# Two state-space scans: rows of B for all sixteen states through TensorE and VectorE, none through the DMA and GpSimd

## The chip, the cores and the metric

The program runs on one core of a Trainium2 chip. The metric is the device time of one execution in microseconds, and the median of three runs is given. The core's engines are TensorE (PE), VectorE (DVE), ScalarE (ACT) and GpSimd (POOL); SyncE (SP) issues DMAs. Each engine works through its own queue in order, and the queues meet at semaphores only.

## What is computed

A decoder of twelve blocks over 16 sequences of 128 rows by 256 columns. Two of the blocks hold a selective scan, and the change touches those two only. Their core, from the reference of the second (`L3_attn`), for every feature f, state n of 16 and row l:

```
A_bar = jnp.exp(-Delta[..., None] * A)
BX = (Delta * h)[..., None] * Bm[:, :, None, :]
_, states = jax.lax.associative_scan(comb, (A_bar, BX), axis=1)    # s[l] = A_bar[l] * s[l-1] + BX[l]
y = jnp.einsum('blfn,bln->blf', states, Cm) + D * h
```

The first (`L1_attn`, a Mamba block with 512 inner features) computes the same kind of scan. B and C are, for every row, 16 numbers each that all features share.

## The kernel before

All twelve blocks are stages of one program. Stage `mamba` (the first scan) works on 4 groups of 4 sequences; a group has 4 blocks of 128 features, taken two at a time as a unit, and each unit goes through the 16 states, so that there are 4 x 2 x 16 = 128 steps. Stage `sequence_ssm` (the second scan) has 256 features, one unit for each of 4 groups, so 64 steps. A step N is, for 128 partitions and two feature blocks of 512 columns:

- `decay` (ACT, L1225): two exponentials; three buffers.
- the drive, dt*x times the row of B. In three steps out of four: `brow` (PE, L1205) spreads the row of B over all partitions into a PSUM bank, with a bf16 matmul against `select`, and `drive` (DVE, L1237) multiplies into another pair of PSUM banks, `c.twins[1]`. In every fourth step (`SHARE = 4`, `shared`): `bload` (SP, L1174) fetches the row by a DMA that repeats it on 128 partitions into `bcol`, and `offer` (POOL, L1261) multiplies into the SBUF tile `offer`.
- `scan` (DVE, L1250): the recurrence over 1024 columns, from decay and drive into one of four `state` buffers. It waits for `summed(N-4)`.
- `crow` (SP, L1169): the row of C by DMA into `ccol`, four buffers; `weigh` (POOL, L1265): state times the row of C, in place.
- `sum` (PE, L1214): adds the weighted state into y, through the identity; four matmul records for a step. The unit's first `sum` also adds the skip term (L1211) and waits for the `finish` of the unit before (`gated`). `finish` (DVE, L1477 and L1780) multiplies y by the gate.

Beside the steps each group needs side work: norm, transposes, projections, the convolution, softplus, and for the group before it the output projection. Its matmuls go through the `side` banks (`Planned`), filled in order; PE waits before it fills a bank again until ACT or DVE has emptied it. The eight PSUM banks are: 0 and 1 for y, 2 and 3 for the drive, 4 for rows of B (one bank), 5 to 7 for side products.

What sets the order: each kind of step has a due number (`MAMBA_BY_STEP` and so on), in units of a step, and `as_due` sorts all of them. Every engine then runs its own share of that list in that order. So a number compares two pieces of work on one engine, not across engines. A bank for rows of B is refilled after the `drive` that reads it (`Fills.before`).

## Time and profile before

| | us |
|---|---|
| median of 3 runs | 3886.33 |
| lowest, highest | 3883.37, 3897.04 |
| the profiled execution | 3884.58 |
| its span in the trace | 3883.2 |
| first scan, first to last scan instruction | 1258.95 to 1808.03 |
| second scan, first to last scan instruction | 3156.74 to 3457.31 |

The profile is of one execution. It has the busy time of each engine, tables of instructions by line with the idle time before them, waits by releaser, and instructions in order of time. A row of a table by line gives the count, total busy time and mean duration in ns, and after the second bar the engine's idle time just before these instructions with what ended it. A row in order of time gives start, duration, engine, line, the operation, how many instructions it merges, and in brackets the idle time before the first. Matmul ends are modelled, and POOL spans are rough.

### The profile page before, as it was taken

The page shows a single profiled execution, that of the slowest core. Times are in us where ns is not written, and L with a number is a line of the kernel's source. Part 1 is how long each engine was busy: PE and PEld are TensorE (multiplying, and loading weights), DVE is VectorE, ACT ScalarE, POOL GpSimd, SP SyncE. Part 2 cuts the span into 40 slices and gives each one's busy share as a digit, 9 for nine tenths or more (in the row PEclk, how much of TensorE's full clock was granted, in tenths as well). Part 3 has the DMA queues.
Part 4 walks back from the last instruction along what each step waited for, and adds up shares of the span by engine and source line. Part 5 has one row for each costly group of instructions (what it writes and reads, how often), then busy time and mean ns, then how long its engine had stood idle before and what let it go on. Part 6 is the DMA issues. An engine that isn't in the chain of part 4 may idle for free. (4 is left out here: it accounts for less than half of the span.)

```text
span 3883.2 us, 52620 instructions
## 1 busy us (share of the span) xinstructions
PE 3058.4 (79%) x17435; PEld 1956.1 (50%) x17435; DVE 2296.3 (59%) x6354; ACT 1543.6 (40%) x3513; POOL 1642.5 (42%) x1169
## 2 busy tenths in 40 slices
PE   6989996878942877865899999478879667768798
PEld 4666665656621332322666666245656423235665
DVE  6998984374333898886244343544542259975553
ACT  4776763211212444431344444315612134426521
POOL 4777774103443888786122222300020157870020
PEclk8999998888976998988999999688969879889999
DMA  3000000202442222222000000111031222220000
GB/s 101 6 10 7 10 10 26 124 22 86 123 119 101 74 68 79 77 74 64 1 8 1 1 1 1 19 71 42 9 120 31 58 75 64 60 79 1 2 1 22
DMA packets 105943, 179.54 MB, mean 46 GB/s; under 512 B 32656, under 2 KB 62376, under 8 KB 102928
## 3 DMA queue, kind: packets, MB, share of 16 engines
q1 hardware_dynamic: 96128, 150.08, 11.9%
q0 software_dynamic: 9552, 26.10, 2.7%
q8 instruction: 148, 2.42, 0.3%
q14 instruction: 115, 0.94, 0.1%
HBM read 151.62 MB, written 24.51 MB: 45 GB/s over the span
## 5 line engine op out<-in xcount | busy, mean ns | idle before, releaser
L1265 POOL TENSOR_TENSOR L_attn_state<-L_attn_state,L_attn_ccol 128x1024 f32<-128x1024 f32 x192 | 533.2, 2791 | 114.5 <-DVE L_attn_state L1250 114.3
L1214 PE MATMUL bank<-L_attn_state,ident 128*128 128x512 f32 x768 | 430.0, 690 | 141.2 <-POOL L_attn_state L1265 140.3
L1225 ACT ACTIVATE L_attn_decay<-L_attn_dt,L_attn_A 128x512 f32<-128x512 f32 x384 | 253.4, 713 | 320.8 <-DVE L_attn_state L1250 291.1
L1214 PEld LDWEIGHTS bank<-L_attn_state,ident 128*128 128x128 f32 x768 | 155.1, 215 | 367.3 <-POOL L_attn_state L1265 224.8
L1250 DVE TENSOR_TENSOR_SCAN L_attn_state<-L_attn_decay,bank 128x1024 f32<-128x1024 f32 x144 | 328.7, 2283 | 14.4 <-ACT L_attn_decay L1225 1.0
L1107 POOL TENSOR_TENSOR L_xattn_prob<-L_xattn_prob,L_xattn_inv 128x1024 f32<-128x1024 f32 x64 | 121.2, 1893 | 408.5 <-DVE L_xattn_inv L1090 408.5
L1237 DVE TENSOR_TENSOR bank<-L_attn_dtx,bank 128x1024 f32<-128x1024 f32 x144 | 175.8, 1221 | 75.2 <-PE bank L1205 55.8
L2831 POOL TENSOR_TENSOR L_attn_t<-L_attn_t,L_attn_base 128x1024 f32<-128x1024 f32 x96 | 182.6, 1902 | 37.7 <-DVE L_attn_base L2780 36.9
L758 ACT ACTIVATE L_xattn_prob<-bank,L_xattn_top 128x128 f32<-128x128 f32 x512 | 142.3, 377 | 56.3 <-DVE L_xattn_top L807 56.0
L2835 POOL TENSOR_TENSOR L_attn_t<-L_attn_t 128x512 f32<-128x512 f32 x96 | 122.1, 1272 | 96.3 <-ACT L_attn_t L2639 96.3
L1032 ACT ACTIVATE L_xattn_prob<-L_xattn_masked,L_xattn_low 128x256 f32<-128x256 f32 x256 | 128.1, 506 | 83.5 <-DVE L_xattn_low L1085 83.5
L1085 DVE CUSTOM_DVE_ANT_0 L_xattn_masked<-bank,L_xattn_hidden 128x256 f32<-128x256 f32 x256 | 96.5, 419 | 105.3 <-PE bank L945 105.3
L2784 DVE MATCH_REPLACE8 L_attn_t<-L_attn_top,L_attn_t 128x64 f32<-128x64 f32 x768 | 150.3, 207 | 0.0
L3484 POOL DMA_INDIRECT L_ffn_xh<-L_ffn_rows,L_ffn_tokens x96 | 90.9, 947 | 136.9 <-PE bank L3289 77.2
L922 PE MATMUL bank<-L_xattn_kvT,L_xattn_wk 128*128 128x256 f32 x512 | 126.1, 389 | 10.8 <-ACT L_xattn_qT L1020 5.1
L931 PE MATMUL bank<-L_xattn_wv,L_xattn_kvT 128*128 128x512 f32 x256 | 126.9, 618 | 2.2 <-DVE L_xattn_kT L987 0.8
L252 POOL TENSOR_TENSOR L_ffn_norm_rs<-L_ffn_norm_mv,eps 128x4 f32<-128x4 f32 x16 | 5.1, 318 | 289.2 <-DVE L_ffn_norm_mv L245 289.2
L1250 DVE TENSOR_TENSOR_SCAN L_attn_state<-L_attn_decay,L_attn_offer 128x1024 f32<-128x1024 f32 x48 | 123.6, 2575 | 0.1
L1205 PE MATMUL bank<-L_attn_parts,L_attn_select 96*128 96x512 bf16 x144 | 61.5, 427 | 74.4 <-DVE bank L1237 72.0
L1261 POOL TENSOR_TENSOR L_attn_offer<-L_attn_dtx,L_attn_bcol 128x1024 f32<-128x1024 f32 x48 | 114.1, 2377 | 0.0
L807 DVE TENSOR_REDUCE L_xattn_top<-bank 128x4 f32<-128x512 f32 x128 | 82.5, 684 | 49.1 <-PE bank L666 49.1
L922 PEld LDWEIGHTS bank<-L_xattn_kvT,L_xattn_wk 128*128 128x128 f32 x512 | 92.1, 190 | 31.9 <-ACT L_xattn_qT L1020 11.5
(601 smaller groups left out, 7481.3 us busy)
## 6 DMA issues: line engine op xcount, KB each, us to landing
L_attn_ccol<-L_attn_bc SPq DMA_DIRECT2D x192, 256.0 KB, 3.2
L_ffn_ew<-in_L_ffn_experts SPq DMA_DIRECT2D x4, 3072.0 KB, 21.3
L_ffn_made<-L_ffn_yout SPq DMA_DIRECT2D x24, 512.0 KB, 3.0
L_attn_bcol<-L_attn_bc SPq DMA_DIRECT2D x48, 256.0 KB, 3.5
L_ffn_w<-in_L_ffn_w SPq DMA_DIRECT2D x4, 2048.0 KB, 14.6
L_xattn_ctx<-in_ctx_rows SPq DMA_DIRECT2D x3, 2048.0 KB, 8.4
L_ffn_rows<-L_ffn_xh SPq DMA_DIRECT2D x8, 512.0 KB, 2.9
L_ffn_made<-L_ffn_yout SPq DMA_DIRECT2D x11, 256.0 KB, 2.1
```

What stands on the lines that cost most here:

```text
L758: t = act.activation(prob[u % 2][j][:, i, :], score[j].bank(u)[:, i * P:(i + 1) * P], ACT.Exp, bias=top[:, j, i:i + 1])
L922: t = pe.matmul(side.bank(at)[:, i * 2 * P:(i + 1) * 2 * P], w["wk"][:, k, col:col + P], kvT[a % 2][:, k, :], start=k == 0, stop=k == KC - 1)
L931: t = pe.matmul(side.bank(at)[:, :], kvT[a % 2][:, k, half * P:(half + 1) * P], w["wv"][:, k, cols], start=k == 0, stop=k == KC - 1)
L1032: t = act.activation(prob[i % 3][:, h, :], masked[i % 2][:, h, :], ACT.Exp, bias=low[:, i % 2, h:h + 1], scale=-1.0, accum_out=total[:, i ...
L1214: t = pe.matmul(self.y[unit % len(self.y)][m][:, :], self.c.ident[:, :], self.state[N % 4][:, m, :], start=False, stop=n == 15)
L1225: t = act.activation(self.decay[N % 3][:, m, :], dt[:, m, :], ACT.Exp, scale=A[:, m, n:n + 1])
L1237: dve.tensor_tensor(self.drive[:, :, :], dtx[:, :, :], self.brow.bank(at)[:, :].unsqueeze(1).broadcast_to([P, 2, GT]), ALU.mult).then_inc( ...
L1250: dve.tensor_tensor_scan(flat(self.state[N % 4]), flat(self.decay[N % 3]), flat(drive), 0.0, ALU.mult, ALU.add).then_inc(*self.scanned.up())
L1265: pool.tensor_tensor(state[:, :, :], state[:, :, :], self.ccol[N % 4][:, :].unsqueeze(1).broadcast_to([P, 2, GT]), ALU.mult).then_inc(*sel ...
L2784: m = dve.match_replace(t[n % RING][:, 1, i, :], top[n % 2][:, i, :], t[n % RING][:, 0, i, :], -1e30)
L2831: pool.tensor_tensor(both, both, base[n % 2][:, :].unsqueeze(1).unsqueeze(3).broadcast_to([P, 2, per, nkeys]), ALU.subtract).then_inc(*shi ...
L2835: pool.tensor_tensor(mine, mine, flat(t[n % RING][:, 1, :, :]), ALU.subtract).then_inc(*picked.up())
```

## The change

The share of drives that went through the DMA and GpSimd is zero in both scans: every step has a `brow` on PE and a `drive` on DVE. `bload` and `offer` and the tiles `bcol` and `offer` are gone. The first scan has two banks for rows of B (4 and 5) and two for side products (6 and 7); the second keeps one (4) and three (5 to 7). The drive keeps its single pair of PSUM banks in both. The tables of due numbers of both stages are new. GpSimd keeps `weigh`, and rows of C still come by DMA.

```diff
-    SHARE = 4
     def shared(self, N):
-        return N % self.SHARE == self.SHARE - 1
+        return self.share and N % self.share == self.share - 1
     def fill(self, N):
-        return (self.SHARE - 1) * (N // self.SHARE) + N % self.SHARE
+        return (self.share - 1) * (N // self.share) + N % self.share if self.share else N
 ...
-            if N:
-                dve.wait_ge(*self.scanned.at(N - 2 if self.shared(N - 1) else N - 1))
+            if N >= len(self.drive):
+                dve.wait_ge(*self.scanned.at(N - len(self.drive)))
 ...
-MAMBA_BY_STEP = {"crow": -4.23, "brow": -2.01, "decay": -1.33, "drive": -0.7, "scan": -0.3, "sum": 0.94, "weigh": 5.35}
-MAMBA_BY_SHARE = {"bload": -5.49, "offer": 4.93}
+MAMBA_BY_STEP = {"crow": -2.17, "decay": -1.75, "brow": -1.71, "drive": 0.2, "scan": 0.95, "weigh": 1.12, "sum": 1.59}
 ...
-    scan = Scan(c, s, w, name, NB, 32, c.banks[4:5], c.banks[0:2], c.twins[1])
+    scan = Scan(c, s, w, name, NB, 32, 0, c.banks[4:6], c.banks[0:2], [s.sb(f"decay{n}", [P, 2, GT]) for n in range(3)], c.twins[1:2])
 ...
-    side = Planned(s, "side", c.banks[5:8], [(step, emptier[step[0]]) for step in order() if step[0] in emptier])
+    side = Planned(s, "side", c.banks[6:8], [(step, emptier[step[0]]) for step in order() if step[0] in emptier])
 ...
-SSM_BY_STEP = {"brow": -1.7, "weigh": -1.61, "drive": -1.01, "crow": -0.46, "decay": -0.43, "scan": -0.41, "sum": 2.11}
-SSM_BY_SHARE = {"bload": -2.46, "offer": -1.97}
+SSM_BY_STEP = {"crow": -3.6, "decay": -1.9, "drive": -1.26, "scan": -0.84, "brow": -0.3, "weigh": -0.22, "sum": 1.97}
 ...
-    scan = Scan(c, s, w, name, KC, 16, c.banks[4:5], c.banks[0:2], c.twins[1])
+    scan = Scan(c, s, w, name, KC, 16, 0, c.banks[4:5], c.banks[0:2], [s.sb(f"decay{n}", [P, 2, GT]) for n in range(3)], c.twins[1:2])
```

TensorE at the end of the first scan, before, first the row of B (`parts`, `select`), then sums of a state; `bank2` names the pair that holds banks 4 and 5:

```order
2708 L1205 MATMUL bank2<-L1_attn_parts1_18119,L1_attn_select3_18124 128x512
2709 L1214 MATMUL bank0<-L1_attn_state0_18128,ident_50 128x512 x2
2710 L1214 MATMUL bank0<-L1_attn_state1_18129,ident_50 128x512 x2
2711 L1205 MATMUL bank2<-L1_attn_parts1_18119,L1_attn_select3_18124 128x512
2712 L1214 MATMUL bank0<-L1_attn_state2_18130,ident_50 128x512 x2
2713 L1205 MATMUL bank2<-L1_attn_parts1_18119,L1_attn_select3_18124 128x512
```

The same place after the change:

```order
2732 L1204 MATMUL bank2<-L1_attn_parts1_18119,L1_attn_select3_18127 128x512
2733 L1213 MATMUL bank0<-L1_attn_state2_18130,ident_50 128x512 x2
2734 L1204 MATMUL bank2<-L1_attn_parts1_18119,L1_attn_select3_18127 128x512
2735 L1213 MATMUL bank0<-L1_attn_state3_18131,ident_50 128x512 x2
2736 L1204 MATMUL bank2<-L1_attn_parts1_18119,L1_attn_select3_18127 128x512
2737 L1213 MATMUL bank0<-L1_attn_state0_18128,ident_50 128x512 x2
```

One row of B stands before each sum now. By the due numbers the row of step N+3 comes before the sum of step N, where it came behind that sum.

GpSimd at the end of the first scan, before: an offer (state 3 of the steps to come) stands ahead of four weighings.

```order
649 L1261 TENSOR_TENSOR L1_attn_offer_18138<-L1_attn_dtx1_18117,L1_attn_bcol1_18137 128x1024
650 L1265 TENSOR_TENSOR L1_attn_state0_18128<-L1_attn_state0_18128,L1_attn_ccol0_18132 128x1024
651 L1265 TENSOR_TENSOR L1_attn_state1_18129<-L1_attn_state1_18129,L1_attn_ccol1_18133 128x1024
652 L1265 TENSOR_TENSOR L1_attn_state2_18130<-L1_attn_state2_18130,L1_attn_ccol2_18134 128x1024
653 L1265 TENSOR_TENSOR L1_attn_state3_18131<-L1_attn_state3_18131,L1_attn_ccol3_18135 128x1024
654 L1261 TENSOR_TENSOR L1_attn_offer_18138<-L1_attn_dtx1_18117,L1_attn_bcol0_18136 128x1024
```

After the change only the weighings are left:

```order
627 L1262 TENSOR_TENSOR L1_attn_state3_18131<-L1_attn_state3_18131,L1_attn_ccol3_18135 128x1024
628 L1262 TENSOR_TENSOR L1_attn_state0_18128<-L1_attn_state0_18128,L1_attn_ccol0_18132 128x1024
629 L1262 TENSOR_TENSOR L1_attn_state1_18129<-L1_attn_state1_18129,L1_attn_ccol1_18133 128x1024
630 L1262 TENSOR_TENSOR L1_attn_state2_18130<-L1_attn_state2_18130,L1_attn_ccol2_18134 128x1024
631 L1262 TENSOR_TENSOR L1_attn_state3_18131<-L1_attn_state3_18131,L1_attn_ccol3_18135 128x1024
```

VectorE in a group of the second scan, before, where the rows of B and C are split into bf16 parts (L1186 to L1195) between scans (L1250) and drives (L1237):

```order
2905 L1762 TENSOR_SCALAR L3_attn_bc_35056<-bank3,L3_attn_b_bc_127 32x512
2906 L1250 SCALAR_TENSOR_TENSOR L3_attn_state2_35075<-L3_attn_decay0_35070,bank1 128x1024
2907 L1250 SCALAR_TENSOR_TENSOR L3_attn_state3_35076<-L3_attn_decay1_35071,L3_attn_offer_35083 128x1024
2908 L1237 TENSOR_TENSOR bank1<-L3_attn_dtx0_35051,bank2 128x1024
2909 L1250 SCALAR_TENSOR_TENSOR L3_attn_state0_35073<-L3_attn_decay2_35072,bank1 128x1024
2910 L1186 CAST L3_attn_parts1_35054<-L3_attn_bc_35056 32x512
```

The same place after the change:

```order
2946 L1754 TENSOR_SCALAR L3_attn_bc_35008<-bank2,L3_attn_b_bc_127 32x512
2947 L1236 TENSOR_TENSOR bank1<-L3_attn_dtx0_35003,bank2 128x1024
2948 L1760 TENSOR_SCALAR L3_attn_d1_35009<-bank3,L3_attn_b_d1_128 16x512
2949 L1185 CAST L3_attn_parts1_35006<-L3_attn_bc_35008 32x512
2950 L1187 TENSOR_TENSOR L3_attn_rest_35035<-L3_attn_bc_35008,L3_attn_parts1_35006 32x512
```

A drive now stands between any two scans, and the split follows one drive behind the rows that it reads.

## Rows read from the trace of the kernel before

**Rows 1.** The page: span, and each engine's busy time and share.
```profile
span 3883.2 us, 52620 instructions
PE 3058.4 (79%) x17435; PEld 1956.1 (50%) x17435; DVE 2296.3 (59%) x6354; ACT 1543.6 (40%) x3513; POOL 1642.5 (42%) x1169
```
**Rows 2.** Windows, first and second scan: length; PE, PEld, DVE, ACT, POOL busy; clock; DMA.
```profile
1257.00:1812.00 555.00, 405.72 (x895) 162.24 (x895) 477.35 (x322) 240.37 (x348) 466.70 (x212) 0.90 0.24 74
3155.00:3462.00 307.00, 231.85 (x545) 96.05 (x545) 278.26 (x271) 124.25 (x195) 255.57 (x134) 0.89 0.21 64
```
**Rows 3.** Table by line, DVE, first scan (1257 to 1812).
```profile
L1250 DVE TENSOR_TENSOR_SCAN L_attn_state<-L_attn_decay,bank 128x1024 f32<-128x1024 f32 x96 | 219.3, 2284 | 11.3 <-ACT L_attn_decay L1225 1.0
L1237 DVE TENSOR_TENSOR bank<-L_attn_dtx,bank 128x1024 f32<-128x1024 f32 x96 | 117.4, 1223 | 67.6 <-PE bank L1205 55.8 <-POOL L_attn_dt L1526 10.7
L1250 DVE TENSOR_TENSOR_SCAN L_attn_state<-L_attn_decay,L_attn_offer 128x1024 f32<-128x1024 f32 x32 | 81.0, 2532 | 0.1
...
L1457 DVE SCALAR_TENSOR_TENSOR L_attn_xc<-bank,L_attn_cols,L_attn_xc 128x504 f32<-128x504 f32 x12 | 8.9, 743 | 0.4
...
L1188 DVE TENSOR_TENSOR L_attn_rest<-L_attn_bc,L_attn_parts 32x512 f32<-32x512 f32 x3 | 8.1, 2714 | 0.1
...
L1193 DVE TENSOR_TENSOR L_attn_rest<-L_attn_rest,L_attn_mid 32x512 f32<-32x512 f32 x3 | 2.0, 679 | 0.0
```
**Rows 4.** Waits of DVE, first scan: total us, times, longest.
```profile
DVE bank L1237 <- PE bank L1205: 55.8, 31, 3.0
...
DVE L_attn_xc L1477 <- PE bank L1214: 5.6, 5, 1.5
```
**Rows 5.** In order of time, the last steps of the first scan, without side work.
```profile
1777.70 6.49 POOL L1265 TENSOR_TENSOR L_attn_state<-L_attn_state,L_attn_ccol 128x1024 f32<-128x1024 f32 x2 [1.33 <-DVE L_attn_state L1250]
...
1781.93 2.73 PE L1214 MATMUL bank<-L_attn_state,ident 128*128 128x512 f32 x4 [3.31 <-POOL L_attn_state L1265]
...
1784.46 0.63 PE L1205 MATMUL bank<-L_attn_parts,L_attn_select 96*128 96x512 bf16 x1
...
1785.19 1.23 DVE L1237 TENSOR_TENSOR bank<-L_attn_dtx,bank 128x1024 f32<-128x1024 f32 x1 [1.92 <-PE bank L1205]
...
1788.88 1.23 DVE L1237 TENSOR_TENSOR bank<-L_attn_dtx,bank 128x1024 f32<-128x1024 f32 x1
...
1790.24 2.29 DVE L1250 TENSOR_TENSOR_SCAN L_attn_state<-L_attn_decay,bank 128x1024 f32<-128x1024 f32 x1
1791.39 1.98 PE L1214 MATMUL bank<-L_attn_state,ident 128*128 128x512 f32 x4 [0.56 <-POOL L_attn_state L1265]
1792.44 2.27 DVE L1250 TENSOR_TENSOR_SCAN L_attn_state<-L_attn_decay,L_attn_offer 128x1024 f32<-128x1024 f32 x1
```
**Rows 6.** In order of time, PE: a slow sum, and an output product after a group.
```profile
1512.77 3.78 PE L1214 MATMUL bank<-L_attn_state,ident 128*128 128x512 f32 x4 [3.48 <-POOL L_attn_state L1265]
...
1549.93 3.69 PE L1366 MATMUL bank<-L_attn_w_out,L_attn_xc 128*128 128x256 f32 x16 [0.83 <-DVE L_attn_xc L1477]
```
**Rows 7.** In order of time, DVE: the last finish of the first scan.
```profile
1818.04 1.23 DVE L1477 TENSOR_TENSOR L_attn_xc<-bank,L_attn_z 128x1024 f32<-128x1024 f32 x1 [7.74 <-PE bank L1214]
```
**Rows 8.** In order of time, DVE: the last finish of the second scan.
```profile
3467.69 1.23 DVE L1780 TENSOR_TENSOR L_attn_h<-bank,L_attn_gate 128x1024 f32<-128x1024 f32 x1 [7.69 <-PE bank L1214]
```
**Rows 9.** Table by line, DVE, second scan (3155 to 3462).
```profile
L1250 DVE TENSOR_TENSOR_SCAN L_attn_state<-L_attn_decay,L_attn_offer 128x1024 f32<-128x1024 f32 x16 | 42.6, 2660 | 0.0
L1751 DVE TENSOR_SCALAR L_attn_cmr<-L_attn_cmv,L_attn_cols 128x4 f32<-128x4 f32 x6 | 8.7, 1453 | 0.2
L1193 DVE TENSOR_TENSOR L_attn_rest<-L_attn_rest,L_attn_mid 32x512 f32<-32x512 f32 x3 | 8.5, 2846 | 0.0
```
**Rows 10.** Waits of DVE, second scan: the first and the last of eight.
```profile
DVE L_attn_d L1768 <- PE bank L1634: 4.9, 3, 2.9
...
DVE L_attn_cbn L1744 <- PE bank L1628: 0.9, 2, 0.7
```
**Rows 11.** Table by line, PE, second scan: the rows of B.
```profile
L1205 PE MATMUL bank<-L_attn_parts,L_attn_select 96*128 96x512 bf16 x47 | 20.0, 425 | 45.9 <-DVE bank L1237 45.7
```

More of the change, by code:

```diff
@@ L1158, in sync @@
                     sp.wait_ge(*self.cgot[last % 4].at(last // 4))
[L1159 to L1160 removed]
+                if self.share:
+                    for last in range(end // self.share - 2, end // self.share):
+                        sp.wait_ge(*self.bgot[last % 2].at(last // 2))
             sp.dma_start(self.kept_rows[N % 2], bc[:, :]).then_inc(*self.kept.up(16))
```

89 lines of the change are left out of this document (40 added, 49 removed).

## The prediction

> **What bounds the kernel now.** I read the page first: over the whole span no engine is full, TensorE 79%, VectorE 59%, GpSimd 42% [rows 1]. The change touches two stages only, so I went to windows over them. They are 555 of 3883 us for the first scan and 307 us for the second [rows 2], and the rest of the program should not move. In the first scan VectorE is busy 477 us (86%) and GpSimd 467 us (84%); in the second 278 us (91%) and 256 us (83%) [rows 2]. Neither view says which one a step waits for last, so the waits of VectorE come next. In the first scan they are 55.8 us for the row of B, in 31 waits of up to 3.0 us, and 5.6 us for the last sum before a finish [rows 4]. In the second scan there is none for a row of B. There are eight small rows, from 4.9 us down to 0.9 us, 21.9 us together, all for side work [rows 10].
>
> The rows in order of time say whose fault the 55.8 us are [rows 5]. TensorE runs a sum at 1781.93 after an idle time of 3.31 us for GpSimd; the row of B stands behind that sum and runs at 1784.46; VectorE starts its drive at 1785.19 after 1.92 us idle. GpSimd is late because two weighings took 6.49 us together, the first of them beside an offered scan, and because each fourth step has an offer too. So in the first scan GpSimd holds up TensorE, TensorE VectorE. In the second VectorE is the bound by itself: TensorE waits 45.7 us for VectorE to free the one bank of B [rows 11].
>
> **The change part by part.** All terms are against the profiled execution, 3884.58 us with a span of 3883.2 us; it lies 1.75 us under the median of the runs, and I add this at the end.
>
> *Drives moved to VectorE.* A step with a drive takes 3.69 us from drive to drive (1785.19 to 1788.88), and one with an offered drive 2.20 us from scan to scan (1790.24 to 1792.44) [rows 5]. The difference, 1.49 us, is 1.22 us of drive [rows 3] and the gaps round it. 32 steps of the first scan cost 32 x 1.49 = +47.7 us, 16 of the second +23.8 us. On VectorE nothing hides this.
>
> *Offered scans.* A scan of an offered drive took 2.53 us in the mean in the first scan [rows 3] and 2.66 us in the second [rows 9]; one that met nothing took 2.27 us [rows 5]. Gone: 32 x 0.26 = 8.3 us and 16 x 0.39 = 6.2 us. The row beside it shows who mostly pays: two weighings in 6.49 us where about 4.7 us would do [rows 5]. The Trainium skill ("SBUF — State Buffer", Who interferes with whom) says that a VectorE instruction with two SBUF inputs and a GpSimd instruction that reads SBUF exclude each other for the whole instruction, and the later one waits. By that rule alone up to 48 x 2.3 = 110 us could come back on VectorE, as an estimate of that page's worst case; the trace agrees on the exclusion but puts the loss on VectorE at 14.5 us, and the sum uses that.
>
> *GpSimd.* It loses 48 offers of 2.35 us, and its weighings are 2.35 us when undisturbed (half of 4.7). In a step of 3.69 us it then has 1.3 us to spare, so the weighing follows its scan at once. Its share of the time falls from 84% to about 64%. Small VectorE operations that wait for it get a little cheaper: L1188 took 2.71 us in the first scan against 0.68 us for the same shape in L1193 [rows 3], L1193 itself 2.85 us in the second, and L1751, on four columns, 1.45 us [rows 9]. That is an excess of about 6 us (3 x 2.03) in the first scan and 14 us (3 x 2.17 and 6 x 1.2) in the second; a quarter of it should go, as GpSimd's share does: -1.5 and -3.5 us.
>
> *Waits for rows of B, first scan.* Two banks, and the row of step N+3 ahead of the sum of step N. I followed one group, with T the end of scan N: weighing to T+2.5, sum to T+4.5 (1.98 us [rows 5]), row N+4 by T+5.6, after drive N+2 has freed its bank; it is wanted at T+11.1. That leaves 5.5 us, and the convolution block costs none of it, since VectorE does 2.2 us of convolution for each block that TensorE makes. After a group's end two output products of 3.69 us [rows 6], a finish and a skip term lie between, and one row comes about 2 us late. At half clock a sum takes 3.78 us [rows 6], which adds about 1 us. I take 3 us for each of three groups and 3 us more, 12 us of waits for 55.8: -43.8 us. The bounds are none left (-55.8) and all left (0, see below). The waits before a finish fall from 5.6 to about 3 us: -2.6 us.
>
> *Waits in the second scan.* One bank here, used each step. In the same reckoning the row N+3 starts when sum N is done, T+4.5, or when drive N+2 is, T+5.0. It ends at T+5.6 and is wanted at T+7.4: a slack of 1.8 us, less than most side products. Followed through a group, this gives 0.5, 0.7, 0.8, 0.4, 1.6, 1.2 and 2.8 us, the last where the projection for B and C waits for the activation and the row of B stands behind it. That is 8 us for each of three groups, and 3 us more for the lower clock, 27 us against 21.9: +5 us. The bounds are 10 us less and 28 us more.
>
> *Ends of the stages.* The last finish comes 7.74 and 7.69 us after the last scan [rows 7, 8], since GpSimd still has two weighings to do. With one left it is 2.4 + 2.0 us and the steps between, 5.0 us: -2.7 us in each.
>
> *Two side banks.* They bind where nothing else runs, before the first drive. The product for a third block must wait for a convolution of three steps of 0.74 us [rows 3], and so must one or two gates: +2.5 us, between 0 and 6 us. In the loop, TensorE stalls up to 3 us in its convolution block, inside the 5.5 us above. The loads of rows of B leave SyncE's queue, where nobody waited for them: 0.
>
> Sum: first scan 47.7 - 8.3 - 1.5 - 43.8 - 2.6 - 2.7 + 2.5 = -8.7 us. Second scan 23.8 - 6.2 - 3.5 + 5 - 2.7 = +16.4 us. Together +7.7 us: 3892.3 us against the profile's own time, 3894 us against the median.
>
> **The rivals.** *A, faster: hardly a wait remains.* Both scans would run at VectorE's own pace: 12 us less in the first scan, and in the second 15 us instead of 27 us. For it: no other engine is over 80% by the sum. Against it: the slack of 1.8 us in the second. 3894 - 24 = 3870 us; with the waits of the second gone too, 3855 us.
>
> *B, slower: the single bank of the second scan.* The place is drive N+3 waiting for row N+3. It decides when TensorE brings it over 1.8 us late: with any side product of four matmuls (about 2 us), and at half clock, where a sum of 3.78 us [rows 6] and a row of 0.63 us [rows 5] fill more than the 3.69 us of a step by themselves. The clock granted in the window is 0.89 of full [rows 2], so about a fifth of the steps. Price: 13 steps x 0.7 us, and 4 groups x 7 side products x 0.7 us more, 28 us: 3922 us. Against it: with the same bank in three of four steps VectorE shows no wait for it now [rows 10], though each fourth step gave it room.
>
> *C, slower: two banks don't help the first scan.* If the rows are late for another reason than the bank, for instance because side products now stall on two banks, the waits stay: +44 us, 3938 us; with half of them (28 instead of 12), 3910 us. The wait came through a sum that waited for GpSimd [rows 5], which speaks against all of it. The Trainium skill ("TensorE: Matmul & The Clock Gate", in its part on thin M) reports a kernel in which double-buffered PSUM gave no further gain. That would be this rival; the present trace neither has two such banks nor settles it.
>
> *D, the moved drives cost nothing*, because VectorE fills its idle time with them. This is A seen from the other side; it needs the 71.5 us of drives to fit in 60 + 29 us of idle time, which only A's orders give.
>
> **How the numbers follow.** Chances: forecast 0.60, A 0.17, B 0.14, C 0.09. The forecast is 3894 us. The range of 8 in 10 takes in A but for its far end, and B but for its last few us: 3866 to 3918 us. About 0.5% (19.4 us) is what a measurement of this kernel can tell from no change, so "same" is 3867 to 3906 us. Faster by more needs the deeper half of A and a little of the forecast, 0.12. Slower by more is B, most of C and the upper edge of the forecast, 0.24. Same is 0.64.
>
> **What would show it.** In the profile after: no L1261 and no offered scan; 192 drives at 1.22 us and 192 scans near 2.28 us; weighings at about 2.4 us in the mean; the last finish 5 us after the last scan. The first scan should last some 12 us less than now and VectorE's waits for rows of B be 8 to 20 us there; in the second the scan lasts 12 to 20 us more. The forecast is wrong if weighings still lag, if the wait for rows of B in the first scan stays over 28 us, or if a new one of over 20 us stands in the second.

## The result, and the profile after the change

| | before | after |
|---|---|---|
| median of 5 runs, us | 3893.38 | 3864.72 |
| lowest, highest | 3883.37, 3899.01 | 3857.68, 3867.3 |
| the profiled execution | 3884.58 | 3857.68 |

After over before is 0.9927, with a 95% interval of 0.9908 to 0.9947: faster by 0.73%. The changed kernel lies 29 us lower, where the forecast (3894 us) was 8 us higher, and just outside the range (3866 to 3918 us).

The page of the changed kernel, as [rows 1]:

```profile
span 3856.4 us, 52617 instructions
PE 3054.9 (79%) x17483; PEld 1954.9 (51%) x17483; DVE 2320.4 (60%) x6402; ACT 1544.4 (40%) x3513; POOL 1449.8 (38%) x1121
```

Windows over the first and the second scan, as [rows 2]: length; busy time of PE, PEld, DVE, ACT, POOL; granted clock; DMA.

```profile
1264.00:1799.00 535.00, 401.16 (x930) 158.12 (x930) 507.67 (x354) 240.09 (x346) 345.39 (x181) 0.95 0.20 62
3135.00:3437.00 302.00, 235.07 (x565) 95.43 (x565) 272.79 (x288) 125.80 (x197) 191.66 (x123) 0.93 0.18 53
```

VectorE is at 95% in the first scan. In the second it has 17 drives more in its window (64 for 47, the window of before missed one) and yet is busy 5.5 us less (272.8 for 278.3). That is the first surprise. The second is in its waits. First scan, as [rows 4]: total us, times, longest.

```profile
DVE bank L1236 <- POOL L_attn_dt L1520: 9.0, 1, 9.0
DVE L_attn_bc L1459 <- PE bank L1346: 3.3, 3, 1.1
DVE L_attn_state L1247 <- ACT L_attn_decay L1224: 1.0, 2, 0.5
```

The 9.0 us are the first drive of the stage. No wait for a row of B is left out of 55.8 us, and none before a finish out of 5.6 us. Second scan, as [rows 10], the rows over 0.9 us; the 7.9 us lie ahead of the first drive, where the window of before did not reach:

```profile
DVE bank L1236 <- PE bank L1204: 10.9, 6, 4.2
DVE bank L1236 <- POOL L_attn_dt L1848: 7.9, 1, 7.9
DVE L_attn_cmr L1748 <- POOL L_attn_crs L1834: 3.1, 3, 1.0
DVE L_attn_whole L1717 <- PE bank L1597: 1.0, 1, 1.0
```

A wait for rows of B is new here (10.9 us), but most of the side-work waits are gone; without the 7.9 us there are 17.8 us where 21.9 stood.

In order of time, the last steps of the first scan, as [rows 5]:

```profile
1765.01 2.29 DVE L1247 TENSOR_TENSOR_SCAN L_attn_state<-L_attn_decay,bank 128x1024 f32<-128x1024 f32 x1
...
1767.34 1.23 DVE L1236 TENSOR_TENSOR bank<-L_attn_dtx,bank 128x1024 f32<-128x1024 f32 x1
...
1767.44 2.35 POOL L1262 TENSOR_TENSOR L_attn_state<-L_attn_state,L_attn_ccol 128x1024 f32<-128x1024 f32 x1 [1.33 <-DVE L_attn_state L1247]
...
1768.62 0.39 PE L1204 MATMUL bank<-L_attn_parts,L_attn_select 96*128 96x512 bf16 x1 [0.47 <-DVE bank L1236]
1768.69 2.29 DVE L1247 TENSOR_TENSOR_SCAN L_attn_state<-L_attn_decay,bank 128x1024 f32<-128x1024 f32 x1
...
1769.85 1.98 PE L1213 MATMUL bank<-L_attn_state,ident 128*128 128x512 f32 x4 [0.83 <-POOL L_attn_state L1262]
...
1771.02 1.23 DVE L1236 TENSOR_TENSOR bank<-L_attn_dtx,bank 128x1024 f32<-128x1024 f32 x1
```

VectorE never idles: drive, scan, drive, 3.68 us a step. A weighing takes 2.35 us and starts 0.1 us after its scan. TensorE makes the row of B as soon as a drive frees a bank, and then the sum.

The last finish of each stage, as [rows 7, 8]:

```profile
1801.39 1.22 DVE L1472 TENSOR_TENSOR L_attn_xc<-bank,L_attn_z 128x1024 f32<-128x1024 f32 x1 [4.63 <-PE bank L1213]
```
```profile
3439.24 1.22 DVE L1772 TENSOR_TENSOR L_attn_h<-bank,L_attn_gate 128x1024 f32<-128x1024 f32 x1 [4.63 <-PE bank L1213]
```

**Where the 27 us of the profiled executions went** (29 in the medians). I cut each stage, by rows in order of time, from its first VectorE instruction (the skip matrices) to the first one of the stage behind it. Prologue is the part up to the first scan instruction, tail the part after the start of the last one.

| us | before | after | difference |
|---|---|---|---|
| up to the first stage (untouched) | 1203.4 | 1207.3 | +3.9 |
| first stage: prologue / scan / tail | 55.5 / 549.1 / 20.0 | 59.7 / 527.5 / 17.2 | -20.2 |
| between the two (untouched) | 1272.3 | 1272.6 | +0.3 |
| second stage: prologue / scan / tail | 56.4 / 300.6 / 18.1 | 52.5 / 295.6 / 14.6 | -12.4 |
| behind the second stage (untouched) | 407.8 | 409.5 | +1.7 |

The untouched part ahead moves by several us from kernel to kernel (1203 to 1218 us over all that follow), so stages are compared by these lengths. The same code of a stage repeats within about 3 us in the first (604.2 to 607.3) and within 5 us in the second (362.6 to 367.3). The profiled execution lies at the lower end of the second: over the other builds of the same code its gain is 8 to 12 us.

### The profile page after: what moved, and what is told of

It reads as the page before. It is cut to its first block and busy times, and to the rows that moved or that the text cites. A ratio compares the mean times of both kernels' runs of the same rounds, so it can differ in the third digit from the quotient of the medians.

```text
span 3856.4 us, 52617 instructions
## 1 busy us (share of the span) xinstructions
PE 3054.9 (79%) x17483; PEld 1954.9 (51%) x17483; DVE 2320.4 (60%) x6402; ACT 1544.4 (40%) x3513; POOL 1449.8 (38%) x1121
## 5 line engine op out<-in xcount | busy, mean ns | idle before, releaser
L1262 POOL TENSOR_TENSOR L_attn_state<-L_attn_state,L_attn_ccol 128x1024 f32<-128x1024 f32 x192 | 451.7, 2354 | 291.4 <-DVE L_attn_state L1247 291.1
L1213 PE MATMUL bank<-L_attn_state,ident 128*128 128x512 f32 x768 | 400.5, 646 | 95.6 <-POOL L_attn_state L1262 95.3
L1247 DVE TENSOR_TENSOR_SCAN L_attn_state<-L_attn_decay,bank 128x1024 f32<-128x1024 f32 x192 | 438.7, 2285 | 20.5 <-ACT L_attn_decay L1224 1.0
L1213 PEld LDWEIGHTS bank<-L_attn_state,ident 128*128 128x128 f32 x768 | 144.4, 201 | 278.4 <-POOL L_attn_state L1262 151.0
L1236 DVE TENSOR_TENSOR bank<-L_attn_dtx,bank 128x1024 f32<-128x1024 f32 x192 | 235.7, 1228 | 34.2 <-PE bank L1204 10.9
L758 ACT ACTIVATE L_xattn_prob<-bank,L_xattn_top 128x128 f32<-128x128 f32 x512 | 141.9, 377 | 56.4 <-DVE L_xattn_top L807 56.0
L1204 PE MATMUL bank<-L_attn_parts,L_attn_select 96*128 96x512 bf16 x192 | 77.9, 406 | 82.1 <-DVE bank L1236 79.2
L1204 PEld LDWEIGHTS bank<-L_attn_parts,L_attn_select 96*128 96x128 bf16 x192 | 19.5, 102 | 188.7 <-DVE bank L1236 160.6
L922 PEld LDWEIGHTS bank<-L_xattn_kvT,L_xattn_wk 128*128 128x128 f32 x512 | 92.3, 190 | 31.8 <-ACT L_xattn_qT L1020 11.5
L2765 DVE TENSOR_TENSOR L_attn_low<-L_attn_top 128x64 f32<-128x64 f32 x96 | 101.2, 1054 | 10.2 <-DVE L_attn_top L2760 0.5
```

The costliest lines, as they stand in the source:

```text
L758: t = act.activation(prob[u % 2][j][:, i, :], score[j].bank(u)[:, i * P:(i + 1) * P], ACT.Exp, bias=top[:, j, i:i + 1])
L922: t = pe.matmul(side.bank(at)[:, i * 2 * P:(i + 1) * 2 * P], w["wk"][:, k, col:col + P], kvT[a % 2][:, k, :], start=k == 0, stop=k == KC - 1)
L1213: t = pe.matmul(self.y[unit % len(self.y)][m][:, :], self.c.ident[:, :], self.state[N % 4][:, m, :], start=False, stop=n == 15)
L1236: dve.tensor_tensor(self.drive[N % len(self.drive)][:, :, :], dtx[:, :, :], self.brow.bank(at)[:, :].unsqueeze(1).broadcast_to([P, 2, GT]) ...
L1247: dve.tensor_tensor_scan(flat(self.state[N % 4]), flat(self.decay[N % len(self.decay)]), flat(self.drive[N % len(self.drive)]), 0.0, ALU.m ...
L1262: pool.tensor_tensor(state[:, :, :], state[:, :, :], self.ccol[N % 4][:, :].unsqueeze(1).broadcast_to([P, 2, GT]), ALU.mult).then_inc(*sel ...
```

## The experiments

Each kernel was timed beside the one of before, whose median was 3888.6 to 3889.8 us. Stage lengths, busy times and waits are from one profiled execution of each.

### One scan at a time

Each kernel has the change in one stage only, and the old class beside the new one for the other. `e1_second_only`:

```diff
-    scan = Scan(c, s, w, name, NB, 32, 0, c.banks[4:6], ...)        # mamba, with the old tables
+    scan = ScanShared(c, s, w, name, NB, 32, c.banks[4:5], c.banks[0:2], c.twins[1])
```

> The first scan's stage is that of the kernel before (offers, its banks and numbers); only the second scan's stage is changed. Theory: the two stages add up, and the second gives about 12 us of the 27 us by which the traces differ, so 12 us less than before (ratio 0.997), with the second stage 363 us long. Rival (my sum on record): the second stage loses 16 us and the first gains more than the trace shows, so this kernel is slower than before, ratio 1.004.

> Only the first scan's stage is changed; the second is that of before. Theory: about 20 us less than before (ratio 0.995), first stage 604 us instead of 625 us, second 375 us as before. Rival: 27 us or more less, with nothing from the second.

Measured: `e1_second_only` 3882.59 us, ratio 0.9982 (0.9973 to 0.9992), stages 623.8 and 363.4 us. `e2_first_only`, the same swap in `sequence_ssm`, 3870.52 us, ratio 0.9955 (0.9939 to 0.9972), stages 604.4 and 375.9 us. Each stage keeps its gain when it is changed alone, within the scatter between builds, so each can be explained by itself. The second scan alone makes the kernel a little faster, where I had it 16 us slower.

### The first scan: bank, order and offers

`e3_one_bank_first` takes the second bank for rows of B back:

```diff
-    scan = Scan(c, s, w, name, NB, 32, 0, c.banks[4:6], ...)
+    scan = Scan(c, s, w, name, NB, 32, 0, c.banks[4:5], ...)
-    side = Planned(s, "side", c.banks[6:8], ...)
+    side = Planned(s, "side", c.banks[5:8], ...)
```

> The changed kernel, but with one bank for rows of B and three for side products in the first scan, with the same numbers. Theory (GpSimd's lag was the cause of the 55.8 us, and not the bank): waits for rows of B in the first scan stay under 15 us, the time is within 10 us of the changed kernel, and the stretch before the first scan gets about 4 us shorter, since the side banks are three again. Rival (the second bank is what removed the waits): 25 to 50 us of waits for rows of B, and the kernel is 20 to 45 us slower than the changed one, so about as slow as before.

Measured: 3939.92 us, ratio 1.0134 (1.0117 to 1.015); first stage 674.2 us for 604.4. The waits of TensorE in its first scan, then those of VectorE:

```profile
PE bank L1204 <- DVE bank L1236: 209.8, 90, 11.7
```
```profile
DVE L_attn_state L1247 <- ACT L_attn_decay L1224: 22.2, 4, 7.3
DVE L_attn_xc L1452 <- ACT L_attn_xc L1389: 18.9, 3, 6.3
DVE L_attn_xc L1472 <- PE bank L1213: 15.9, 7, 2.3
DVE bank L1236 <- PE bank L1204: 12.8, 8, 3.9
```

In the new order the row of B stands ahead of the sum. With one bank TensorE sits there until a drive frees it, 90 times and up to 6.7 us in the steps (the 11.7 us is the wait for the stage's first drive; the change has one of 11.5 us), and holds up the side products behind it. What VectorE then lacks is hardly the row itself (12.8 us) but the side work: decays, convolution, sums. The new order is 70 us worse than with the second bank, more than either expectation had, and the 12.8 us of waits for rows would by themselves have spoken for the first. Three side banks shorten the prologue by 2.8 us (56.9 for 59.7).

`e4_before_order` goes further: the drives are moved, but banks and numbers are those of before in both scans (in the second the row's number had to go from -1.7 to -0.7).

```diff
-MAMBA_BY_STEP = {"crow": -2.17, "decay": -1.75, "brow": -1.71, "drive": 0.2, "scan": 0.95, "weigh": 1.12, "sum": 1.59}
+MAMBA_BY_STEP = {"crow": -4.23, "brow": -2.01, "decay": -1.33, "drive": -0.7, "scan": -0.3, "sum": 0.94, "weigh": 5.35}
 ...
-    scan = Scan(c, s, w, name, NB, 32, 0, c.banks[4:6], ...)
+    scan = Scan(c, s, w, name, NB, 32, 0, c.banks[4:5], ...)
 ...
-SSM_BY_STEP = {"crow": -3.6, "decay": -1.9, "drive": -1.26, "scan": -0.84, "brow": -0.3, "weigh": -0.22, "sum": 1.97}
+SSM_BY_STEP = {"brow": -0.7, "weigh": -1.61, "drive": -1.01, "crow": -0.46, "decay": -0.43, "scan": -0.41, "sum": 2.11}
```

> All drives on VectorE, but banks and numbers of the kernel before in both scans (without the offers; in the second scan rows of B one step later, -0.7 for -1.7, since one bank cannot run as far ahead when it is used every step). Theory (moving the drives frees GpSimd and that gives most of the gain of the first scan): first scan's waits for rows of B under 20 us, time 0 to 15 us less than before. In the second scan the small VectorE operations with SBUF operands stay as long as before (20 us of excess), since they follow a scan, so the second stage is 5 to 15 us longer than before. Rival (the order alone matters): first scan as slow as before plus 48 us of drives.

Measured: 3936.86 us, ratio 1.0128 (1.0111 to 1.0145). The first stage takes 625.0 us, as before (624.6): VectorE is busy 31.6 us more in its scan (508.9 for 477.4) and waits 25.8 us for rows of B, 30 us less. In this scan the moved drives alone fill idle time and cost nothing. The second stage, expected 5 to 15 us longer, takes 420.8 us for 375.0 (waits for rows of B 39.5 us); one number differs there from both kernels, so this size belongs to that kernel alone. VectorE's waits for side work there are 24.9 us, about as before.

`e7_offers_new_order` is the opposite: the kernel of before, with its offers and banks, and the new numbers (the offer and its load are given places among them).

```diff
-MAMBA_BY_SHARE = {"bload": -5.49, "offer": 4.93}
+MAMBA_BY_SHARE = {"bload": -2.6, "offer": 0.7}
 ...
-SSM_BY_SHARE = {"bload": -2.46, "offer": -1.97}
+SSM_BY_SHARE = {"bload": -2.6, "offer": -0.6}
```

> The kernel before (offers on GpSimd, one bank for rows of B, three for side products) with the numbers of the changed kernel; offers placed one step's part ahead of the weighing of the same four steps. Theory (GpSimd's load with offers is the bound of the first scan): the waits for rows of B stay over 30 us in the first scan, and the kernel is within 12 us of before; the second scan gains about 10 us since the small operations are moved. Rival (the order was it): as fast as the changed kernel or faster, since VectorE has 71 us less to do.

Measured: 3908.93 us, ratio 1.005 (1.0033 to 1.0068); stages 616.8 and 391.3 us. In its first scan the waits for rows of B fall to 8.4 us, where over 30 were expected: so even with offers the new numbers remove most of them. The time comes back elsewhere, as the table by line shows, VectorE:

```profile
L1250 DVE TENSOR_TENSOR_SCAN L_attn_state<-L_attn_decay,L_attn_offer 128x1024 f32<-128x1024 f32 x32 | 90.9, 2840 | 0.0
L261 DVE TENSOR_SCALAR L_attn_xn<-X,L_attn_norm_mv,L_attn_norm_rs 128x256 f32<-128x256 f32 x12 | 17.6, 1530 | 0.0
```

An offered scan takes 2.84 us (2.53 in [rows 3]), the norm of L261 1.53 us (0.81 before), and a finish waits 17.0 us for sums in all (5.6 in [rows 4]). The second stage is 16 us longer than before, not 10 us shorter. I set the places of the offers once and did not vary them. `e9_offers_two_banks` adds the second bank, with the second scan as in the change:

```diff
-    scan = Scan(c, s, w, name, NB, 32, 0, c.banks[4:6], ...)
+    scan = ScanShared(c, s, w, name, NB, 32, c.banks[4:6], c.banks[0:2], c.twins[1])
```

> First scan: offers stay with GpSimd as before, but two banks for rows of B, two for side products and the numbers of the changed kernel; the second scan is the changed one. Theory A (moving the drives is worth something in the first scan, because GpSimd's lag ends): first stage about 610 to 618 us, so 6 to 14 us slower than the changed kernel. Rival B (the second bank and the numbers did it all, the moved drives only cost their 48 us minus what they free): first stage 590 to 603 us, faster than the changed kernel.

Measured: 3872.41 us, ratio 0.9952 (0.9937 to 0.9967); first stage 614.9 us. With offers the second bank gives 2 us, without them 70. So with two banks and the new numbers, and with the offers where I had put them, an offer in every fourth step costs the first scan 10.5 us (614.9 for 604.4) more than a drive on VectorE does. Over that stage 32 drives fewer are 40.1 us less for VectorE, but its offered scans take 17.9 us and its small operations 15.7 us longer in all, and it is idle 17.1 us more.

`e10_two_banks_before_numbers` has moved drives and two banks, with the old numbers in the first scan. `e11_row_behind_sum` and `e12_before_numbers_row_first` exchange one number: the first takes it from the change, the second gives it to `e10`.

```diff
-MAMBA_BY_STEP = {"crow": -2.17, "decay": -1.75, "brow": -1.71, ...      # e11, the rest as after
+MAMBA_BY_STEP = {"crow": -2.17, "decay": -1.75, "brow": -1.35, ...
 ...
-MAMBA_BY_STEP = {"crow": -4.23, "brow": -2.01, "decay": -1.33, ...      # e12, the rest as e10
+MAMBA_BY_STEP = {"crow": -4.23, "brow": -2.1, "decay": -1.33, ...
```

> First scan: drives on VectorE and two banks for rows of B and two for side products as in the changed kernel, but the due numbers of the kernel before; the second scan is the changed one. Theory (two banks remove the waits, and the numbers only matter with one): waits for rows of B under 8 us in the first scan, first stage 600 to 612 us. Rival (the row of B has to be ahead of the sum, or side products stall on two banks with the old numbers): 15 us of waits or more, first stage 615 to 630 us.

> The changed kernel with one number of the first scan back to the order of before: the row of B of step N+3 stands just behind the sum of step N on TensorE (brow -1.35), no longer just ahead of it (-1.71). Two banks, moved drives, all other numbers as in the change. Theory 1 (the row's place makes the second bank pay): VectorE waits for rows of B again, 10 to 30 us, first stage 615 to 635. Theory 2 (the side work's place does it, the row's place matters little with two banks): first stage 604 to 608.

> The first scan of the kernel with moved drives, two banks for rows of B, two for side products and the numbers of before (first stage 638.6, waits for rows of B 28.2, TensorE held up by side banks), with the row of B moved ahead of the sum alone (brow -2.1 instead of -2.01). Theory 1 (the row's place): most of the 34 us between 638.6 and 604.4 comes back, first stage 605 to 620. Theory 2 (the side work's place): it stays at 630 to 640. The second scan is that of the change.

Measured: `e10` 3897.28 us, 1.0023 (1.0009 to 1.0036); `e11` 3882.77 us, 0.9982 (0.997 to 0.9995); `e12` 3883.19 us, 0.9982 (0.9973 to 0.9991). The first stage, in us:

| moved drives, two banks | row of B behind the sum | ahead of it |
|---|---|---|
| all other numbers of before | 638.6 (`e10`) | 622.8 (`e12`) |
| all other numbers of the change | 622.5 (`e11`) | 604.4 (after) |

`e10` was slower than both of its expectations: with 28.2 us of waits for rows of B, two banks do not remove the waits by themselves. Of the two theories on `e11` and `e12` both are half right. The row's place gives 16 to 18 us, the other numbers as much again, and they add up. In `e12` the row passes hardly anything but the sum; in `e11` it also falls behind seven side products of each group, so `e12` is the cleaner of the two. Each has its own wait. In `e11` VectorE waits for rows of B as it did before, in small pieces, because the sum ahead of the row waits for GpSimd (VectorE's and then TensorE's waits, first scan):

```profile
DVE bank L1236 <- PE bank L1204: 20.9, 13, 2.3
```
```profile
PE bank L1213 <- POOL L_attn_state L1262: 134.6, 81, 5.5
```

In the change that second row reads 65.9 us, longest 2.0. In `e12` TensorE is held up by the two side banks instead, 28.1 us in three rows, where the change has one such row of 4.2 us. What VectorE then lacks are rows of B again and a convolution input:

```profile
PE bank L1333 <- DVE L_attn_xc L1452: 10.9, 5, 3.6
PE bank L1333 <- DVE X L1479: 9.5, 2, 4.7
PE bank L1333 <- ACT L_attn_z L1396: 7.7, 3, 2.6
```
```profile
PE bank L1333 <- DVE L_attn_xc L1452: 4.2, 3, 1.7
```
```profile
DVE bank L1236 <- PE bank L1204: 11.6, 3, 4.4
...
DVE L_attn_xc L1452 <- ACT L_attn_xc L1389: 4.9, 2, 2.6
```

So the other numbers are what lets the side work live on two banks. The first scan in one table, stage lengths in us:

| banks for rows of B, numbers | with offers | drives moved |
|---|---|---|
| one, before | 624.6 (before) | 625.0 (`e4`) |
| one, new | 616.8 (`e7`) | 674.2 (`e3`) |
| two, before | not run | 638.6 (`e10`) |
| two, new | 614.9 (`e9`) | 604.4 (after) |

### The second scan: where small operations stand

`e5_side_after_scan` moves three numbers so that the small VectorE operations of each group stand just behind a scan again, not behind a drive:

```diff
-                "normal": (-9.86, -7.98), ... "back0": -7.91, ... "split": -5.89,
+                "normal": (-9.83, -7.82), ... "back0": -7.75, ... "split": -5.8,
```

> The changed kernel with three numbers of the second scan moved by less than 0.2 of a step, so that the split, the second block's statistics and back0 come just behind a scan on VectorE and not just behind a drive. Nothing else changes. Theory (these operations are blocked by the weighing, which starts when a scan ends): their time in the second scan goes up by 8 to 20 us (rows L1192 to L1194 and L1743 to 1.3 us and more above their own), and the kernel is 5 to 18 us slower than the changed one. Rival (they are shorter because GpSimd is less busy at all times): no change beyond 3 us.

Measured: 3883.77 us, ratio 0.9988 (0.9974 to 1.0001); second stage 382.3 us for 362.7, VectorE busy 287.9 us for 272.8. In order of time, VectorE and GpSimd, first in `e5`, then in the change:

```profile
3205.52 2.27 DVE L1247 TENSOR_TENSOR_SCAN L_attn_state<-L_attn_decay,bank 128x1024 f32<-128x1024 f32 x1
...
3207.93 2.39 POOL L1262 TENSOR_TENSOR L_attn_state<-L_attn_state,L_attn_ccol 128x1024 f32<-128x1024 f32 x1 [8.02 <-DVE L_attn_state L1247]
3208.14 2.73 DVE L1187 TENSOR_TENSOR L_attn_rest<-L_attn_bc,L_attn_parts 32x512 f32<-32x512 f32 x1
```
```profile
3185.72 2.35 POOL L1262 TENSOR_TENSOR L_attn_state<-L_attn_state,L_attn_ccol 128x1024 f32<-128x1024 f32 x1 [1.33 <-DVE L_attn_state L1247]
...
3187.55 1.23 DVE L1236 TENSOR_TENSOR bank<-L_attn_dtx,bank 128x1024 f32<-128x1024 f32 x1 [1.34 <-PE bank L1204]
...
3189.79 0.68 DVE L1187 TENSOR_TENSOR L_attn_rest<-L_attn_bc,L_attn_parts 32x512 f32<-32x512 f32 x1
```

A scan's end starts a weighing. A small operation with two SBUF inputs close behind the scan is caught by it and takes 2.73 us, up to 0.55 us past the weighing's end (3210.32). In the change the weighing is over, since a wait of 1.34 us, a drive and L1760 lie between. A drive alone is too short for that: in the first scan of the change the cast L1185 stands right behind a drive, is issued with 1.32 us of a weighing still to run, and takes 1.60 us for 0.42.

That GpSimd has fewer instructions is not the main cause: in `e4`, with the offers gone too but the old order, L1187 still took 2.72 us and L1185 2.23 us, and in `e7`, with the offers kept but the new order, three of the four lines that the change shortens are as short as in the change. Second scan, VectorE, before and then `e7`:

```profile
L1195 DVE CAST L_attn_parts<-L_attn_rest 32x512 bf16<-32x512 f32 x3 | 7.4, 2458 | 0.1
L1186 DVE CAST L_attn_parts<-L_attn_bc 32x512 bf16<-32x512 f32 x3 | 3.8, 1276 | 0.0
```
```profile
L1193 DVE TENSOR_TENSOR L_attn_rest<-L_attn_rest,L_attn_mid 32x512 f32<-32x512 f32 x3 | 2.0, 679 | 0.0
...
L1195 DVE CAST L_attn_parts<-L_attn_rest 32x512 bf16<-32x512 f32 x3 | 1.3, 417 | 0.1
...
L1186 DVE CAST L_attn_parts<-L_attn_bc 32x512 bf16<-32x512 f32 x3 | 1.2, 403 | 0.0
```

The fourth, L1751, went only from 1.45 to 1.08 us there, and to 0.25 us in the change. Nor was it always a weighing that caught them before: L1193 met the GpSimd instruction that finishes dt for the next group (L1848), and L1195 an offer; L1186 and L1751 met weighings. In order of time, before, VectorE and GpSimd:

```profile
3217.92 2.35 POOL L1848 TENSOR_TENSOR L_attn_dt<-L_attn_dt,L_attn_soft 128x1024 f32<-128x1024 f32 x1 [1.72 <-ACT L_attn_soft L1703]
3217.97 2.84 DVE L1193 TENSOR_TENSOR L_attn_rest<-L_attn_rest,L_attn_mid 32x512 f32<-32x512 f32 x1
...
3220.24 2.79 POOL L1261 TENSOR_TENSOR L_attn_offer<-L_attn_dtx,L_attn_bcol 128x1024 f32<-128x1024 f32 x1
...
3220.85 2.46 DVE L1195 CAST L_attn_parts<-L_attn_rest 32x512 bf16<-32x512 f32 x1
```

`e8_two_banks_second` gives the second scan two banks and two:

```diff
-    scan = Scan(c, s, w, name, KC, 16, 0, c.banks[4:5], ...)
+    scan = Scan(c, s, w, name, KC, 16, 0, c.banks[4:6], ...)
-    side = Planned(s, "side", c.banks[5:8], ...)
+    side = Planned(s, "side", c.banks[6:8], ...)
```

> The changed kernel with two banks for rows of B and two for side products in the second scan too. Theory: the 10.9 us of waits for rows of B there fall to about 3 us, but the stretch before its first scan gets some us longer and side products wait more, so 0 to 6 us faster than the changed kernel. Rival (the side banks bind): 5 to 15 us slower.

Measured: 3871.95 us, ratio 0.9958 (0.9943 to 0.9973); second stage 366.8 us, waits for rows of B 12.6 us. The waits did not fall to 3 us as expected and the stage gained nothing, so with this order the bank is not what they come from. The kernel as a whole is 7 to 10 us above the two medians of the change; in the profiles that excess lies mostly in code that the edit does not touch (8 to 10 us ahead of the first stage, 3 us in it). In this scan's new numbers the row of step N+3 stands behind the sum of step N; that side products ahead of the row make it late is my reading of the order, and was not tested.

### The exclusion itself

`e6_drive_in_sbuf` puts the drive into an SBUF tile in both scans, so that each scan reads two SBUF inputs:

```diff
-    scan = Scan(..., c.twins[1:2])
+    scan = Scan(..., [s.sb("drive0", [P, 2, GT])])
```

> The changed kernel with the drive written to an SBUF tile and not to PSUM banks, in both scans, so that every scan has two SBUF inputs. Theory (VectorE with two SBUF inputs and GpSimd exclude each other): scan and weighing cannot overlap, a step takes 2.28 + 2.35 = 4.6 us or more and not 3.69, so 192 x 0.9 = about 175 us slower, with scans or weighings well over 2.4 us in the mean. Rival (the two offered scans' excess had another cause): no change beyond 10 us.

Measured: 4041.77 us in one run, 177 us above the change (about 175 expected); stages 717.6 and 424.3 us. In order of time at the end of the first scan:

```profile
1891.47 1.22 DVE L1236 TENSOR_TENSOR L_attn_drive<-L_attn_dtx,bank 128x1024 f32<-128x1024 f32 x1
1891.58 2.36 POOL L1262 TENSOR_TENSOR L_attn_state<-L_attn_state,L_attn_ccol 128x1024 f32<-128x1024 f32 x1 [2.29 <-DVE L_attn_state L1247]
...
1892.82 3.26 DVE L1247 TENSOR_TENSOR_SCAN L_attn_state<-L_attn_decay,L_attn_drive 128x1024 f32<-128x1024 f32 x1
```

The scan is issued at 1892.82, the weighing ends at 1893.94, the scan 2.14 us after that, where an undisturbed scan takes 2.28 us: it did next to nothing until the weighing was over. The same holds for all 131 scans of that kernel that were issued with over 0.2 us of a weighing still to run: each ended 2.14 to 2.15 us after the weighing. A step takes 4.65 us (drive at 1891.47, the next at 1896.12) instead of 3.68. This is what the Trainium skill says ("SBUF — State Buffer", Who interferes with whom): the two exclude each other for the whole instruction and the later one waits. The trace agrees here, and shows how the price is set: not a whole weighing, but the 1.1 us of it still to run when the scan is issued.

### Two later numbers

`g1_later_split` moves the split of the second scan later, and in the first scan the work on rows of B and C before the steps; `g2_later_rows_first` has the first-scan part alone; `after_again` is the changed kernel once more.

```diff
-                  "delta": -14.77, "keep": -14.57, "projected": -14.5, "rows": -13.24,      # g1 and g2
+                  "delta": -14.77, "keep": -9.7, "projected": -14.5, "rows": -9.75,
 ...
-                "ranks": -6.2, ... "split": -5.89, "rank": -5.56,                           # g1 only
+                "ranks": -5.8, ... "split": -5.25, "rank": -5.28,
```

> The changed kernel with five due numbers moved. Second scan: rank behind the row of B of the next step, ranks behind the scan, split behind the next drive. First scan: rows and keep just ahead of split, so that the first cast comes 0.7 us later behind a scan. Theory: waits for rows of B in the second scan fall from 10.9 to about 5 us, the first scan's cast L1185 from 1.6 to about 0.9 us and its waits for the projection (3.3 us) go, so 5 to 10 us less than the changed kernel. Rival (what follows the split then comes late): 0 to 10 us more, with a new wait for parts or for the decay.

> The changed kernel with two numbers of the first scan moved: rows of B and C are stored and kept later (rows -9.75, keep -9.7 instead of -13.24 and -14.57). The kernel with this and a later split in the second scan had the first stage at 599.6 (after: 604.4). If those two numbers did it, the first stage is 599 to 601 here, and the kernel 3 to 5 us under the changed one (3853 to 3858); if it was scatter between builds, 603 to 605 and no difference.

> The changed kernel once more, unchanged, beside the three others of this call. Expected as measured before: ratio 0.991 to 0.995, first stage 604, second stage 363 to 367. It says how far two runs of the same code are apart, and is what the other three are held against.

Measured: `g1` 3859.43 us, 0.9931 (0.9909 to 0.9953), stages 599.6 and 366.3; `g2` 3861.06 us, 0.9922 (0.9909 to 0.9936), first stage 599.6; `after_again` 3862.11 us, 0.9925 (0.9911 to 0.9938), first stage 604.2. The first stage is 4.6 us shorter in both: the 3.3 us of waits at L1459 are gone, and 2 us of blocked operations (VectorE busy 505.7 for 507.7). The whole time does not show it, 1 us in 3862 with overlapping intervals. The cast L1185, issued 0.7 us later, takes 0.89 us in `g1` and `g2`, for 1.60. I count it as a gain of a stage, not as a faster kernel. The later split of the second scan, in `g1` alone, did not do what I expected: waits for rows of B are 13.7 us there, not 5, and the stage is no shorter.

## Why the prediction was wrong

What it said of the moved work held. A step is 3.68 us (forecast 3.69), the 48 former offered scans cost 14.0 us less (7.9 and 6.1; forecast 14.5), weighings are 2.35 us, and the last finishes come 2.8 and 3.5 us earlier (forecast 2.7). Of the three signs by which the forecast was to be known as wrong none came: the weighings don't lag, and the waits for rows of B are none and 10.9 us. It failed on the other side, where I had named no sign. The offered scans gave back 14.0 us, as the sum had it, and far from the worst case of 110 us; but the small operations gave 27.8 us (5.4 and 22.4), where the sum had 5.

| term | forecast, us | measured |
|---|---|---|
| first: drives moved | +47.7 | +47.7 (not measured by itself; pace 3.68 for 3.69) |
| offered scans | -8.3 | -7.9 |
| small operations | -1.5 | -5.4 |
| waits for rows of B | -43.8 | -55.8 |
| waits before a finish | -2.6 | -5.6 |
| tail | -2.7 | -2.8 |
| two side banks, prologue | +2.5 | +4.2 |
| wait at L1459 | none | +3.3 |
| second: drives moved | +23.8 | +23.8 (not measured by itself) |
| offered scans | -6.2 | -6.1 |
| small operations | -3.5 | -22.4 |
| waits | +5 | -4.1 |
| tail | -2.7 | -3.5 |
| prologue | none | -3.9 |

The measured terms add to -22.3 us in the first stage and -16.2 us in the second, against -20.2 and -12.4 by stage; 2 and 4 us are short gaps that I have not named. The untouched code added another 6 us. In the first scan the 6.1 us that L1188 lost are partly offset by the cast ahead of it (L1185), which took 3.6 us more: it is now issued behind a drive, while it was issued just before the weighing began.

**The step that failed most: "a quarter of it should go, as GpSimd's share does".** For the small operations that wait for GpSimd I took the loss as a matter of chance, in proportion to GpSimd's share of the time. The rows say otherwise. In the second scan this term alone is 19 of the 35 us between the sum (+7.7) and the profiled execution (-26.9). Table by line of the second scan, VectorE, to set against L1751 and L1193 in [rows 9]:

```profile
L1192 DVE TENSOR_TENSOR L_attn_rest<-L_attn_rest,L_attn_mid 32x512 f32<-32x512 f32 x3 | 2.0, 680 | 0.0
...
L1743 DVE TENSOR_SCALAR L_attn_cmr<-L_attn_cmv,L_attn_cols 128x4 f32<-128x4 f32 x6 | 1.5, 248 | 0.2
```

Over all four groups 6.5 and 7.2 us are gone from these two, and 6.1 and 2.6 us from L1195 and L1186 of before. I had counted the excess of L1193 and L1751 only, and had missed the other two lines. In the order shown ahead of the prediction, the change's split stands behind a drive where it stood behind a scan; I printed it and drew nothing from it. `e5` puts small operations back behind a scan, though in part others (L1187, L1748 and L1743): 15 us more of VectorE's busy time and 15 to 20 us more of the stage (382.3 for 362.7 to 367.3). That it is a matter of what GpSimd runs when each is issued is shown by this and by `e7`, where the new numbers gave back 15.2 of the 22.4 us with the offers still on GpSimd; for L1751 the two causes are not separated.

**The waits, first scan.** The reason was right, its size not: my hand-followed group left 3 us per group for late rows and 3 us for the clock, and none came. The lower bound I had set (-55.8 us) is what happened. The sum credited all of it to the second bank and the row's place; but with the moved drives alone 30 of the 55.8 us are gone (`e4`), and with the new numbers alone 47 (`e7`). The granted clock was 0.95 and 0.93, not the 0.90 and 0.89 of before [rows 2], and I had charged 3 us in each scan for the lower one; that the higher clock saved them is likely, not shown. That bank, row's place and the other numbers are all needed I had not seen. Rival C, that two banks don't help, was right only of the kernel with the old numbers (`e10`: 638.6 us).

**The waits, second scan.** The sum put 27 us of waits for rows of B (24 and 3 for the clock) in place of the 21.9 us of before, and had no term for side work at all. Measured are 10.9 us in six waits for rows and 6.9 us for side work. With the old numbers and moved drives (`e4`) the waits for side work stay at 24.9 us. Rival B priced the single bank at 28 us above that; `e8` shows no cost of this bank.

The time came out between the two prices of rival A, 3870 and 3855 us, to which I had given 0.17. That is partly luck: A's fewer waits are 21 us of the gap (12.0 and 9.1), and the rest is mostly the small operations, which A does not contain. For the waits, I let the worst place of one hand-followed group stand for all. What remains open: which of the other numbers of the first scan makes the two side banks suffice (the 16 to 18 us between `e10` and `e11`), and why the prologue of the second stage is shorter (52.5 to 54.1 us over the builds, for 56.4 and 57.0 with the code of before).

## What to carry to other kernels

Work that is moved onto the fullest engine can cost nothing while that engine waits for the one it is taken from, as in the first scan (625.0 for 624.6 us); first ask what the waits are for, then where the time would go. A second buffer and an order that uses it are one change: the order without the bank lost 49 us, the bank without the order 14 us, both together won 21 us. Small SBUF operations on VectorE belong where GpSimd has nothing to run: read, for each, which GpSimd instruction is running when it is issued and how much of it is left (here 2.2 us close behind a scan, still 1.3 us right behind a drive), and not GpSimd's average share.

## What of the hardware was not expected

- The price of the exclusion between VectorE and GpSimd is what the GpSimd instruction still has to run when the VectorE one is issued, less about 0.13 us for the scans and the operations on 32x512: 0.68 us became 2.73 us for an operation issued 0.21 us after a weighing had begun (`e5`), and a scan of 2.28 us became 3.26 us when issued 1.24 us after (`e6`, and so within 0.01 us for 131 scans). It is not for two SBUF inputs alone: a cast of 0.42 us with 1.32 us of a weighing to run took 1.60 us, by the same sum. Before the change it was mostly GpSimd that paid: its 127 weighings took 2.77 us in the mean, 2.35 us after.

```profile
L1265 POOL TENSOR_TENSOR L_attn_state<-L_attn_state,L_attn_ccol 128x1024 f32<-128x1024 f32 x127 | 350.6, 2773 | 70.9 <-DVE L_attn_state L1250 70.9
```
```profile
L1262 POOL TENSOR_TENSOR L_attn_state<-L_attn_state,L_attn_ccol 128x1024 f32<-128x1024 f32 x128 | 301.2, 2354 | 187.7 <-DVE L_attn_state L1247 187.6
```

- The granted clock of TensorE in the first scan differed from kernel to kernel at nearly the same work: 0.90 with 406 of 555 us busy before, 0.95 with 401 of 535 us after, 0.94 in `e11` (394 of 552), 0.89 in `e10` (416 of 567) and in `e9` (405 of 542), 0.90 in `e3` (402 of 607) and 0.84 in `e6` (456 of 646). It does not simply follow the length of the scan; whether it is cause or effect of a smooth order no run here separates.
- Double buffering in PSUM was worth 70 us in one scan with the order made for it, 21 us against the better of the two one-bank kernels with moved drives (`e4`), and nothing in the other scan. The Trainium skill ("TensorE: Matmul & The Clock Gate", HAM oscillation — how this bites in real kernels) tells of one kernel, of another kind, where it gave no further gain; here the second scan did likewise, the first did not. In the first, `e3` shows why it matters there: the row of B ahead of the sum makes TensorE stand still for the bank. The second was not run with that order.
